# Mixture of experts for two images: router in one stage, experts as one pipeline of 36 tiles, weights turned tile by tile

## The reference

```python
t = t + _L2_ffn_ref(_ln_t(t), router_w, router_b, expert_w, expert_b)

def _L2_ffn_ref(x, router_w, router_b, expert_w, expert_b):
    router_probs = softmax(x @ router_w + router_b, axis=-1)
    top_p, top_i = top_k(router_probs, 2)
    top_p = top_p / sum(top_p, axis=-1, keepdims=True)
    expert_out = einsum('bnd,edc->bnec', x, expert_w) + expert_b
    gathered = take_along_axis(expert_out, top_i[..., None], axis=2)
    return einsum('bnk,bnkc->bnc', top_p, gathered)
```

## Time and profile before

| | us |
|---|---|
| timed runs, median of 3 | 8045.21 |
| lowest and highest | 8036.98, 8050.74 |
| the profiled execution | 8063.09 |
| its span, first to last instruction | 8061.3 |

### The profile page before, as it was taken

One profiled execution on the slowest core, in us unless ns is written; L12 is line 12 of the kernel. 1 busy time (PEld: TensorE's weight loads), 2 busy tenths in 40 slices (PEclk: granted clock), 3 DMA queues, 4 the chain that ended last, 5 costly groups with the idle time before them and its releaser, 6 DMA issues. The chain is left out here.

```text
span 8061.3 us, 170699 instructions
## 1 busy us (share of the span) xinstructions
PE 7207.0 (89%) x62518; PEld 6199.1 (77%) x62522; DVE 5978.0 (74%) x9091; ACT 4073.4 (51%) x8517; POOL 3649.1 (45%) x4036
## 2 busy tenths in 40 slices
PE   7999889998999989999756788879897999999999
PEld 6888668886788867888546666635666989989899
DVE  7999879997899978999644555445556767767677
ACT  5888568885688757887312222124443222222222
POOL 4888558885688846888355545411000000000000
PEclk9999999999999999999878899889998999999999
DMA  2333223232233312333365555400003434434343
GB/s 62 91 93 93 72 62 92 92 90 68 68 90 94 92 58 76 92 93 89 103 177 169 163 158 144 118 6 3 1 0 95 128 115 124 124 115 123 116 124 111
DMA packets 590233, 762.33 MB, mean 95 GB/s; under 512 B 51687, under 2 KB 527880, under 8 KB 587569
## 3 DMA queue, kind: packets, MB, share of 16 engines
q1 hardware_dynamic: 537777, 584.54, 24.4%
q0 software_dynamic: 51840, 169.91, 7.4%
HBM read 720.59 MB, written 33.66 MB: 94 GB/s over the span
## 5 line engine op out<-in xcount | busy, mean ns | idle before, releaser
L630 POOL TENSOR_TENSOR l_arena<-l_arena 128x768 f32<-128x768 f32 x1536 | 2589.9, 1687 | 454.4 <-DVE l_arena L562 447.8
L562 DVE TENSOR_TENSOR_SCAN l_arena<-l_arena,psum 128x772 f32<-128x772 f32 x1536 | 2663.7, 1750 | 176.7 <-PE psum L394 72.6
L487 ACT ACTIVATE l_arena<-l_arena,l_A 128x384 f32<-128x384 f32 x3072 | 1642.5, 603 | 36.2 <-DVE l_arena L562 32.8
L396 PE MATMUL psum<-l_arena 128*128 128x128 f32 x11520 | 1498.6, 280 | 46.9 <-DVE l_arena L562 43.3
L396 PEld LDWEIGHTS psum<-l_arena 128*128 128x128 f32 x11520 | 1366.8, 192 | 170.7 <-issue 147.1
L407 PE MATMUL psum<-l_ident,l_arena 128*128 128x128 f32 x9216 | 1257.5, 273 | 50.5 <-ACT l_yT L493 41.6
L407 PEld LDWEIGHTS psum<-l_ident,l_arena 128*128 128x128 f32 x9216 | 1055.2, 141 | 60.2 <-POOL l_arena L630 60.2
L2256 POOL TENSOR_TENSOR st_mab<-st_xr 128x384 f32<-128x384 f32 x8 | 7.9, 1003 | 2055.8 <-DVE st_xr L2246 2055.8
L1189 POOL DMA_INDIRECT l_G<-neighbours,l_idx x648 | 617.3, 953 | 677.1 <-PE psum L1237 324.9
L477 ACT ACTIVATE l_arena<-l_arena,l_BT 128x256 f32<-128x256 f32 x1728 | 746.7, 496 | 7.5
L2531 ACT ACTIVATE st_own_s<-psum 128x384 f32<-128x384 f32 x256 | 125.5, 490 | 1089.9 <-PE psum L2368 1089.9
(11 more groups left out here) (438 smaller groups left out, 11300.3 us busy)
## 6 DMA issues: line engine op xcount, KB each, us to landing
l_arena<-c_rows SPq DMA_DIRECT2D x1536, 192.0 KB, 3.0
st_FS<-filter_sums SPq DMA_DIRECT2D x128, 1155.0 KB, 9.3
st_F<-filter_parts SPq DMA_DIRECT2D x128, 320.5 KB, 7.1
neighbours<-l_xt SPq DMA_DIRECT2D x256, 72.0 KB
st_mab<-in_st_mp SPq DMA_DIRECT2D x68, 256.0 KB, 9.3
st_mab<-in_st_mm SPq DMA_DIRECT2D x68, 256.0 KB, 6.1
l_G<-neighbours,l_idx POOLq DMA_INDIRECT x648
l_gnx<-in_x SPq DMA_DIRECT2D x4, 1152.0 KB, 5.5
```

Of the source, the lines that this page charges most:

```text
L396: mm = pe.matmul(ps[:, o:o + P], dtuT[:, g % 2, t, h * P:(h + 1) * P], diagB[:, rank[s] % 3, t, :], start=True, stop=True)
L487: act.activation(decay[:, s % NDC, half(h)], dtv[:, g % 2, h, :], ACT.Exp, scale=A[:, g // NRC, h, n:n + 1]).then_inc(s_exp, 1)
L562: dve.tensor_tensor_scan(hbuf[:, n, run], decay[:, s % NDC, run], x2_ps[s % 2][:, run], 0.0, ALU.mult, ALU.add).then_inc(s_scan, 1)
L630: pool.tensor_tensor(hC[:, s % NHC], halves(hbuf[:, s % NS, :]), Cs[:, s % NCS, :].unsqueeze(1).broadcast_to([P, 2, RC]), ALU.mult).then_i ...
```

## The change

Three things change in `layer2_experts`:

- The router's logits of both images are made in one stage without the copy `xb`: TensorE reads `xn` directly, and each image's logits go to a bank of their own.
- The experts of both images become one pipeline over 36 tiles in one stage, written out, with no loop over images. The copies to `xb` and `wb` are gone; `xn` and `s1` are read directly.
- The weights are no longer turned for a whole image ahead of its pipeline. TensorE turns the weights of tile t right behind the experts of tile t (`turn_weights`), and ScalarE copies each tile's 8 x 128 to one of four buffers of `wT`. The mix of tile t waits for that copy, the turn of tile t for the copy of tile t-2, and ScalarE's copy of tile t for the mix of tile t-4.

```diff
--- before.py
+++ after.py
@@ -1664,16 +1664,16 @@
         rw, rb, rb_all, ones_r = sb("rw", [P, NE]), sb("rb", [1, NE]), sb("rb_all", [P, NE]), sb("ones_r", [1, P])
         ew, eb = sb("ew", [P, NE * C]), sb("eb", [NE, C])
         ones_c, ident, order = sb("ones_c", [P, P]), sb("ident", [P, P]), sb("order", [P, NE])
-        xb, wb, wT = sb("xb", [P, L]), sb("wb", [P, TB, NE]), sb("wT", [NE, L])
+        wT = sb("wT", [NE, 4, P])
         lg, sc, s1, s2 = (sb(n, [P, tiles, NE]) for n in ("lg", "sc", "s1", "s2"))
         m1, m2 = sb("m1", [P, tiles, 1]), sb("m2", [P, tiles, 1])
         ep = sb("ep", [P, 3, NE, C])
         loads = [(rw[:], w["rw"]), (rb[:], w["rb"]), (ew[:], w["ew"]), (eb[:], w["eb"]),
                  (ones_c[:], w["ones_c"]), (ident[:], w["ident"]), (order[:], w["order"])]
-        s_w, s_one, s_bs, s_xb, s_lg, s_lc, s_v, s_e = (sem(n) for n in (
-            "loaded", "ones", "bias_spread", "x_copied", "logits", "logits_copied", "dve", "exp"))
-        s_xb2, s_wt, s_wc, s_ex, s_mul, s_half, s_pr, s_o, s_res = (sem(n) for n in (
-            "x_copied2", "weights_turned", "weights_copied", "experts", "weighted", "halved", "quartered", "mixed", "residual"))
+        s_w, s_one, s_bs, s_lg, s_lc, s_v, s_e = (sem(n) for n in (
+            "loaded", "ones", "bias_spread", "logits", "logits_copied", "dve", "exp"))
+        s_wt, s_wc, s_ex, s_mul, s_half, s_pr, s_o, s_res = (sem(n) for n in (
+            "weights_turned", "weights_copied", "experts", "weighted", "halved", "quartered", "mixed", "residual"))
         with nc.Block() as block:
             @block.sync
             def _(sp):
@@ -1698,20 +1698,20 @@
                 pool.wait_ge(s_w, 16 * len(loads))
 
         normalize(nc, ctx, sem, "mo_ln", ps, xres, xn, ones_c[:], w["eps5"], NI * L // BANK)
-        with nc.Fori(0, NI) as b:
-            with nc.Block() as block:
-                @block.vector
-                def _(dve):
-                    dve.tensor_copy(xb[:], xn[:, ds(b * L, L)]).then_inc(s_xb, 1)
+        with nc.Block() as block:
+            @block.vector
+            def _(dve):
+                for b in range(NI):
                     dve.wait_ge(s_lg, b + 1)
-                    dve.tensor_tensor(lg[:, ds(b * TB, TB), :], ps[:, 0:TB * NE].rearrange("p (t e) -> p t e", e=NE),
+                    dve.tensor_tensor(lg[:, b * TB:(b + 1) * TB, :], ps[:, BANK * b:BANK * b + TB * NE].rearrange("p (t e) -> p t e", e=NE),
                                       rb_all[:].unsqueeze(1).broadcast_to([P, TB, NE]), ALU.add).then_inc(s_lc, 1)
 
-                @block.tensor
-                def _(pe):
-                    pe.wait_ge(s_xb, b + 1)
+            @block.tensor
+            def _(pe):
+                for b in range(NI):
                     for t in range(TB):
-                        mm = pe.matmul(ps[:, t * NE:(t + 1) * NE], xb[:, t * P:(t + 1) * P], rw[:], start=True, stop=True)
+                        n = b * TB + t
+                        mm = pe.matmul(ps[:, BANK * b + t * NE:BANK * b + (t + 1) * NE], xn[:, n * P:(n + 1) * P], rw[:], start=True, stop=True)
                     mm.then_inc(s_lg, 1)
 
         with nc.Block() as block:
@@ -1749,82 +1749,73 @@
                 act.wait_ge(s_v, 2)
                 act.activation(lg[:], lg[:], ACT.Exp).then_inc(s_e, 1)
 
-        with nc.Fori(0, NI) as b:
-            with nc.Block() as block:
-                @block.vector
-                def _(dve):
-                    dve.tensor_copy(xb[:], xn[:, ds(b * L, L)])
-                    dve.tensor_copy(wb[:], s1[:, ds(b * TB, TB), :]).then_inc(s_xb2, 1)
-
-                    def residual(t):
-                        dve.wait_ge(s_o, b * TB + t + 1)
-                        xs = xres[:, ds(b * L + t * P, P)]
-                        dve.tensor_tensor(xs, xs, ps[:, BANK * (4 + t % 2):BANK * (4 + t % 2) + P], ALU.add).then_inc(s_res, 1)
-
-                    dve.wait_ge(s_xb2, b + 1)
-                    for t in range(TB + 3):
-                        if t < TB:
-                            dve.wait_ge(s_ex, b * TB + t + 1)
-                            if t >= 3:
-
-                                dve.wait_ge(s_o, b * TB + t - 2)
-                            dve.tensor_tensor(ep[:, t % 3], ps[:, 2 * BANK * (t % 2):2 * BANK * (t % 2) + NE * C].rearrange("p (e c) -> p e c", e=NE),
-                                              wb[:, t, :].unsqueeze(2).broadcast_to([P, NE, C]), ALU.mult).then_inc(s_mul, 1)
-                        if 1 <= t <= TB:
-
-                            u = t - 1
-                            dve.wait_ge(s_half, b * TB + u + 1)
-                            dve.tensor_tensor(ep[:, u % 3, 0:2], ep[:, u % 3, 0:2], ep[:, u % 3, 2:4], ALU.add).then_inc(s_pr, 1)
+        with nc.Block() as block:
+            @block.vector
+            def _(dve):
+                def residual(t):
+                    dve.wait_ge(s_o, t + 1)
+                    xs = xres[:, t * P:(t + 1) * P]
+                    dve.tensor_tensor(xs, xs, ps[:, BANK * (4 + t % 2):BANK * (4 + t % 2) + P], ALU.add).then_inc(s_res, 1)
+
+                for t in range(tiles + 3):
+                    if t < tiles:
+                        dve.wait_ge(s_ex, t + 1)
                         if t >= 3:
-                            residual(t - 3)
-
-                @block.gpsimd
-                def _(pool):
-                    for t in range(TB):
-                        pool.wait_ge(s_mul, b * TB + t + 1)
-                        pool.tensor_tensor(ep[:, t % 3, 0:4], ep[:, t % 3, 0:4], ep[:, t % 3, 4:8], ALU.add).then_inc(s_half, 1)
-
-                @block.scalar
-                def _(act):
-                    for q in range(NRC):
-                        act.wait_ge(s_wt, b * NRC + q + 1)
-                        act.activation(wT[:, q * RC:(q + 1) * RC], ps[0:NE, BANK * (6 + q % 2):BANK * (6 + q % 2) + RC],
-                                       ACT.Copy).then_inc(s_wc, 1)
-
-                @block.tensor
-                def _(pe):
-                    pe.wait_ge(s_xb2, b + 1)
-                    for q in range(NRC):
-                        if q >= 2:
-                            pe.wait_ge(s_wc, b * NRC + q - 1)
-                        for t in range(RC // P):
-                            o = BANK * (6 + q % 2) + t * P
-                            mm = pe.matmul(ps[0:NE, o:o + P], wb[:, q * (RC // P) + t, :], ident[:], start=True, stop=True)
-                        mm.then_inc(s_wt, 1)
-
-                    def mix(t):
-                        pe.wait_ge(s_pr, b * TB + t + 1)
+
+                            dve.wait_ge(s_o, t - 2)
+                        dve.tensor_tensor(ep[:, t % 3], ps[:, 2 * BANK * (t % 2):2 * BANK * (t % 2) + NE * C].rearrange("p (e c) -> p e c", e=NE),
+                                          s1[:, t, :].unsqueeze(2).broadcast_to([P, NE, C]), ALU.mult).then_inc(s_mul, 1)
+                    if 1 <= t <= tiles:
+
+                        u = t - 1
+                        dve.wait_ge(s_half, u + 1)
+                        dve.tensor_tensor(ep[:, u % 3, 0:2], ep[:, u % 3, 0:2], ep[:, u % 3, 2:4], ALU.add).then_inc(s_pr, 1)
+                    if t >= 3:
+                        residual(t - 3)
+
+            @block.gpsimd
+            def _(pool):
+                for t in range(tiles):
+                    pool.wait_ge(s_mul, t + 1)
+                    pool.tensor_tensor(ep[:, t % 3, 0:4], ep[:, t % 3, 0:4], ep[:, t % 3, 4:8], ALU.add).then_inc(s_half, 1)
+
+            @block.scalar
+            def _(act):
+                for t in range(tiles):
+                    act.wait_ge(s_wt, t + 1)
+                    if t >= 4:
+                        act.wait_ge(s_o, t - 3)
+                    act.activation(wT[:, t % 4, :], ps[0:NE, BANK * (6 + t % 2):BANK * (6 + t % 2) + P], ACT.Copy).then_inc(s_wc, 1)
+
+            @block.tensor
+            def _(pe):
+                def turn_weights(t):
+                    if t >= 2:
+                        pe.wait_ge(s_wc, t - 1)
+                    pe.matmul(ps[0:NE, BANK * (6 + t % 2):BANK * (6 + t % 2) + P], s1[:, t, :], ident[:], start=True, stop=True).then_inc(s_wt, 1)
+
+                def mix(t):
+                    pe.wait_ge(s_wc, t + 1)
+                    pe.wait_ge(s_pr, t + 1)
+                    if t >= 2:
+                        pe.wait_ge(s_res, t - 1)
+                    dst = ps[:, BANK * (4 + t % 2):BANK * (4 + t % 2) + P]
+                    pe.matmul(dst, eb[:], wT[:, t % 4, :], start=True, stop=False)
+                    for e in range(2):
+                        mm = pe.matmul(dst, ep[:, t % 3, e, :], ident[:], start=False, stop=(e == 1))
+                    mm.then_inc(s_o, 1)
+
+                for t in range(tiles + 2):
+                    if t < tiles:
                         if t >= 2:
-                            pe.wait_ge(s_res, b * TB + t - 1)
```

(27 more changed lines are left out.)

## The result

Nine runs of each kernel, taken together: the changed kernel's median is 8023.58 us, the kernel before's 8037.37 us, 13.8 us apart. Executions with a fallen granted clock (here one of the changed kernel, 8576.72 us; later one each in two other kernels) stand in the medians but not in the ratios. The ratio is 0.9977 with a 95% interval of 0.9968 to 0.9986, so by it the change saves 0.23%, some 18.5 us (11 to 26), where 6.1 us had been forecast. Part of that is the starting point: the three runs of the kernel before that were known then had a median 8 us above that of the nine.

The account below looks back on a forecast made before the run. TensorE sets the experts' pace. Router gain 4.0 us plus experts' 2.1 (120.5 for 122.65: 0.6 + 2.4 + 102.0 + 14.7 + 0.8) makes 6.1, so 8045.2 - 6.1 = 8039.1 us; range 8025 to 8052.

Parts of the forecast that it names:

- these 153 us: From the norm's end to layer 3's attention, about 1.9% of the span; all the change's effect was expected inside it.
- Rival (d): Experts' pipeline: something such as a straight-line code fetch holds TensorE at tile 18; up to 9 us return, about 8048; chance 0.06.
- The turn, 0.42 us a tile: Experts' pipeline: 0.22 us of passes plus 0.20 for one more change of stationary shape, over 35 tiles 14.7 us.
- the start of the experts: Between the choice's end and TensorE's first expert pass: the meeting of the engines, taken as 0.6 us.
- The router, 4.0 us: Router's stretch: both images' logits in one stage take 16.8 us in place of 20.81, clock kept low.
- Rival (b): Router: its matmuls catch the clock at 2.4 GHz and keep it; gain up to 14.0 us, time 8031.2; chance 0.10.
- The opening, 2.4 us at the low clock: Experts' first passes: half the work is lost until the clock rises, 2.4 us, kept between 1.6 and 3.4.
- The closing term: End of the experts' pipeline: 0.8 us more, kept from the second image's slower last tiles at the low clock.
- No hole at tile 18: Sign in the new pipeline's profile: TensorE passes from the first image's tiles to the second's without a gap.
- The pipeline of 102.0 us without turns: Experts: the first image's 52.15 us for 18 tiles plus 18 more at 2.77 us, 49.9, makes 102.0 for 36.
- The base: Starting time of the forecast: the median of three timed runs of the kernel before, 8045.21 us.

Follow-up runs that it names:

- four turns: The changed kernel with the turn and ScalarE's copy for the first four tiles only, later tiles using those stale weights; 7975.78 us, ratio 1.0258.
- the wide turn: The changed kernel with a 128-column stationary for the turn (the tile's 8 weights and those of the 15 tiles after it); timed once, 8051.60 us.
- the router alone: The kernel before with only the changed kernel's one-stage router, the experts' loops kept; 7954.19 us, ratio 1.0234.
- put back in place: The kernel before with the one-stage router only, plus 153 instructions of fulfilled waits on TensorE moving the last layer's long loop; 7770.34 us, ratio 1.0001.
- the seam kept: The kernel before with the one-stage router and weights turned tile by tile, but the two loops' stages over images and copies kept; 7958.36 us, ratio 1.0238.

## Why the prediction was wrong

- **"The prediction is wrong if the stage before or after these 153 us moves, which nothing in the change gives a reason for."** This is the step that failed. The change gives a reason: it makes code longer and shorter, and all that stands behind it moves. The last layer fell by 8.7 us in the profile, and most of that is the place of VectorE's code: 16 instructions of waits gave the kernel before 7.9 of them, and 112 took 6.5 of them from the changed kernel. The profiles show this; the timed ratios of those kernels are too wide for it. It is nearly half of the 19.5 us that the two profiles show as gained, and it is no merit of the change but luck. On TensorE the same thing was worth 185 us the other way, and the changed kernel missed it by its place, 154 of 256. Rival (d) named a fetch of straight-line code, and looked for it inside the new pipeline, where no run shows one (2.77 and 3.09 us a tile to the end).
- **The turn, 0.42 us a tile.** Measured 0.32. The mechanism was right and the term mis-sized. A change of shape costs 0.09 us before the first pass. It costs another 0.10 before the second where the new stationary is the bias product's 8 x 128 or the identity's 128 x 128 behind it; but the second pass of the 128 x 8 turn comes after 0.11, as if nothing had changed. I had given every change the price of the bias product's. 35 x 0.10 is 3.5 of the 4.7 us by which the stretch gained more than forecast; 0.8 are the router's, and 0.3 the start of the experts (0.3 us for 0.6).
- **The router, 4.0 us.** Measured 4.8: 0.3 us to TensorE's first pass in place of 0.6, and 0.59 as the mean clock of the first 3 us. Rival (b) came true for a few passes, worth well under a microsecond.
- **The opening, 2.4 us at the low clock.** It was low for 5.0 us from the first pass, half of which is 2.5. Right. The closing term stood too: of the 116.5 us from the first expert pass (5355.31) to the last residual (5471.84), 102.0, the turns' 11.2 and this 2.5 leave 0.8. That the clock rose and fell there about as before is not the change's doing; over the kernels here it moved that part by up to 2 us.
- **No hole at tile 18.** Right: rival (d) as it was priced did not happen, and the seam's removal is worth 8.6 us by the kernel that keeps it.
- **The pipeline of 102.0 us without turns.** With four turns the part from the choice's end was 106.4; less 0.3, 2.3 (the clock low for 4.5 us), the closing 0.8 and some 1 us for the four turns, that is 102.0. Right.
- **The base.** The forecast was a difference, and put on the median of three runs it became a time 8 us too high. With the base of nine runs the same difference would give 8031.3, and the measured time would lie inside a range of the same width (8017 to 8044). The difference was short by more than half all the same: 6.1 for 13.8 by the medians and 18.5 by the ratio. What the two profiles show beyond the forecast is 4.7 us in this stretch and 8.7 in the last layer.

The Trainium skill's "TensorEngine Tiling (Array Packing)", Key Properties, says that a change of tiling mode drains the engine. The traces agree with it for the first pass behind each change (0.09 to 0.1 us, gone in the wide turn). The Trainium skill's "TensorE: Matmul & The Clock Gate", Step-by-step, says that the next weights are loaded while the present matmul runs. Here the passes follow without a pause, 0.11 or 0.43 us apart, only between equal shapes and at the second pass of the narrow turn; no row shows whether it is the load that the others wait for.

## What to carry to other kernels

A small matmul put between large ones costs its passes in full where TensorE is the bound, and 0.1 to 0.2 us for each edge at which the stationary's shape changes (the turn's edge cost 0.1, the two of the bias product 0.38 together, 2.77 for 2.39); pad the small operands to the large ones' shape, or gather many of them into one. When a change moves the time by two or three per cent or less, compare the stages whose code is the same, and the packets of the instruction queues: a loop whose code moved can give or take more than the change itself. Before judging such a kernel, shift its later code with a few fulfilled waits and look whether the verdict stays.

## What the runs showed of the hardware

With a loop of 1670 instructions on TensorE the last layer took 170 to 225 us more than the 2007 of the kernel before, with 215 more packets of 16 KB, when it began at 241, 245 or 26 inside a piece of 256 instructions, and was quick at 144, 154, 158, 159 and 180. On VectorE an outer loop of 322 instructions waited up to 7.1 us at each jump back when it began at 29 of 128, and did not at 45 (270 or 271 packets of 8 KB, and 255). The three kernels in which it began at 20 or 21 (the router alone, put back in place, the seam kept) have 270 packets too, and waits of up to 6.2 us. No place between 29 and 45 was run, and what the fetching engine keeps is not settled by these runs. The gathers of layers 1 and 2 took 977 to 980 us in two batches of runs and 1259 to 1277 in the others, with the same code, on different chips; that is open too.
